# A float32 attention and mixture-of-experts kernel: the moving operand and the output of its split products are walked in pairs of columns

## The reference, cut to what matters

```python
q = query + braak_embed[braak_stages][..., None]
attn = softmax(einsum('bsd,btd->bst', q, key)); o = einsum('bst,btd->bsd', attn, value)
t = rms_norm(o) * norm_w
weights = top2(softmax(t @ gate_w.T))
h1 = (t @ w1.T)[None] + 2.0 * einsum('etr,efr->etf', einsum('td,erd->etr', t, a1), b1)
h3 = (t @ w3.T)[None] + 2.0 * einsum('etr,efr->etf', einsum('td,erd->etr', t, a3), b3)
act = silu(h1) * h3
out_e = einsum('etf,df->etd', act, w2) + 2.0 * einsum('etr,edr->etd', einsum('etf,erf->etr', act, a2), b2)
out = x + einsum('te,etd->td', weights, out_e)
```

## Time and profile before

| | |
|---|---|
| timed executions, median of 2 | 1308.16 us |
| profiled execution | 1308.66 us |
| its span | 1306.9 us |
| TensorE matmuls, records | 7286 |
| granted TensorE clock over the span | 1.00 of full speed |
| VectorE busy | 65% |
| ScalarE busy | 40% |
| DMA over the span | 53 GB/s |

### The profile page before, as it was taken

The page is one execution under the profiler, slowest core; times in us unless marked ns, Lnnn a source line. Parts: engine busy times, 40 slices in busy tenths (PEclk is TensorE's granted clock), DMA queues, the critical chain, the costliest instruction groups (busy, mean ns, idle before and its releaser), DMA issues.

```text
span 1306.9 us, 18607 instructions
## 1 busy us (share of the span) xinstructions
PE 1301.1 (100%) x7286; PEld 1139.3 (87%) x7286; DVE 843.5 (65%) x1558; ACT 527.5 (40%) x991; POOL 249.9 (19%) x213
## 2 busy tenths in 40 slices
PE   9999999999999999999999999999999999999998
PEld 8999998888888888888888888888888888888887
DVE  6776656756665576656675667557675666565556
ACT  6776753333343344333333334333333343243332
POOL 3556540202011020202020202011020202020200
PEclk9999999999999999999999999999999999999999
DMA  9555810020202020201102020202020101102000
GB/s 294 145 147 154 233 43 33 2 73 2 73 2 73 1 73 1 59 16 33 42 2 73 1 73 2 73 1 74 2 73 1 57 17 35 40 1 73 1 17 17
DMA packets 71791, 69.56 MB, mean 53 GB/s; under 512 B 7050, under 2 KB 62744, under 8 KB 71576
## 3 DMA queue, kind: packets, MB, share of 16 engines
q1 hardware_dynamic: 71392, 68.37, 17.5%
q10 hardware_dynamic: 312, 0.02, 0.0%
HBM read 51.27 MB, written 17.10 MB: 52 GB/s over the span
## 4 chain that ended last, share of the span: by engine, by line
PE 98%; ACT 1%; DVE 0%; issue 0%; DVEq 0%
PE bank L1205 31%; PE bank L1204 31%; PE bank L1206 30%; PE bank L1330 2%; PE bank L1257 2%; PE bank L1308 1%; PE bank L1250 1%; ACT prob L663 0%; PE bank L1216 0%; ACT qT_hi L646 0%; ACT kT_hi L647 0%; DVE probT_lo L886 0%; DVE x_out L1148 0%; PE bank L1295 0%; ACT value_hi L657 0%
## 5 line engine op out<-in xcount | busy, mean ns | idle before, releaser
L1076 DVE TENSOR_TENSOR act_a<-silu_a,bank 128x512 f32<-128x512 f32 x128 | 87.7, 686 | 210.9 <-PE bank L1206 194.2
L754 ACT ACTIVATE br_hi<-act_br 128x512 fp32r<-128x512 f32 x128 | 81.0, 633 | 188.6 <-DVE act_br L1087 188.6
L747 ACT ACTIVATE silu_b<-bank 128x512 f32<-128x512 f32 x128 | 76.3, 596 | 187.9 <-PE bank L1206 187.0
L590 POOL TENSOR_TENSOR t_lo<-t_in,t_hi 128x512 fp32r<-128x512 f32 x32 | 40.6, 1291 | 552.2 <-ACT t_hi L734 552.2
L1205 PE MATMUL bank<-w2T_lo,s_hi 128*128 128x256 f32 x512 | 144.7, 283 | 0.0
L1206 PE MATMUL bank<-w2T_hi,s_lo 128*128 128x256 f32 x512 | 143.3, 280 | 0.0
L1204 PE MATMUL bank<-w2T_hi,s_hi 128*128 128x256 f32 x512 | 142.7, 279 | 0.0
L1084 DVE TENSOR_TENSOR act_b<-silu_b,bank 128x512 f32<-128x512 f32 x128 | 88.0, 688 | 81.4 <-PE bank L1206 80.4
L743 ACT ACTIVATE silu_a<-bank 128x512 f32<-128x512 f32 x128 | 75.8, 592 | 134.1 <-PE bank L1206 134.0
L609 POOL TENSOR_TENSOR v_lo<-v_full,v_hi 128x512 fp32r<-128x512 f32 x64 | 94.5, 1508 | 136.6 <-ACT v_hi L739 136.6
L1097 DVE TENSOR_TENSOR br_lo<-act_br,br_hi 128x512 fp32r<-128x512 f32 x128 | 104.7, 818 | 5.6 <-ACT br_hi L754 3.1
(11 more groups left out here) (197 smaller groups left out, 3242.2 us busy)
## 6 DMA issues: line engine op xcount, KB each, us to landing
kv<-in_fside_BxSxS SPq DMA_DIRECT2D x32, 256.0 KB, 3.3
x_in<-in_x SPq DMA_DIRECT2D x32, 256.0 KB, 4.0
t_scratch<-oT SPq DMA_DIRECT2D x32, 256.0 KB, 2.5
t_in<-t_scratch SPq DMA_DIRECT2D x16, 512.0 KB
x_out<-in_x SPq DMA_DIRECT2D x16, 512.0 KB, 4.0
out<-x_out SPq DMA_DIRECT2D x30, 256.0 KB, 4.0
rho<-scale_scratch SPq DMA_DIRECT2D x16, 256.0 KB
rstd<-scale_scratch SPq DMA_DIRECT2D x16, 256.0 KB
```

Source lines behind the costliest of these rows:

```text
L747: nc.scalar.activation(silu_b[:, :], h1_bank[j % 2][:, :], ACT.Silu).then_inc(silu_b_ready, 1)
L754: nc.scalar.activation(br_hi[j % 2][:, :], act_br[j % 2][:, :], ACT.Copy).then_inc(br_hi_ready, 1)
L1076: nc.vector.tensor_tensor(act_a[j % 2][:, :], silu_a[j % 2][:, :], h3_bank[j % 2][:, :], ALU.mult).then_inc(act_a_ready, 1)
```

## The change

One line is added to `product`. The output and both parts of the moving operand are rearranged, all in the same way, before the three matmuls are issued. With N columns, the order becomes 0, 1, N/2, N/2 + 1, 2, 3, N/2 + 2, N/2 + 3, and so on: two neighbouring columns (8 bytes) of the first half, two of the second half, by turns. Since the output is walked in the same order as the moving operand, every value lands where it did before. The stationary operand and its load are as before.

```diff
             def product(dst, w, x_parts, start, stop, grouped=True):
 
                 (w_hi, w_lo), (x_hi, x_lo) = w, x_parts
+                dst, x_hi, x_lo = (part.rearrange("p (a b c) -> p b a c", a=2, c=2) for part in (dst, x_hi, x_lo))
                 nc.tensor.matmul(dst, w_hi, x_hi, start=start, stop=False, skip_group_check=not grouped)
                 nc.tensor.matmul(dst, w_hi, x_lo, start=False, stop=False, skip_group_check=not grouped)
                 return nc.tensor.matmul(dst, w_lo, x_hi, start=False, stop=stop, skip_group_check=not grouped)
```

## The result

The changed kernel took 1859.72 us (median of 2, 1859.07 to 1860.38) against 1308.16 us: ratio 1.421, 95% interval 1.418 to 1.425. It is slower by 42%, where 3.8% faster was forecast. Its profiled execution has a span of 1857.3 us, 550.4 us more than before.

What follows compares the result with a forecast made beforehand. TensorE's matmul distances were taken to bound the kernel; savings of 35.1, 2.8, 10.4 and 2.3 us summed to 50.6 us, bringing the median from 1308.16 to 1258 us, 3.8% faster. The range was 1238 to 1395 us.

Steps and rivals of the forecast that it cites:

- What bounds the kernel: Whole span: TensorE's matmul start distances set the time; excess over streaming the columns totals 81 us.
- Is the excess a fixed price or a stall: Matmuls in `product`: the 13.4 ns excess at 512 columns is mostly a stall between moving read and weight load.
- The read: Moving operand from SBUF: pairs by turns remove most of the stall, giving 218 ns for 512 columns, 111.5 for 256.
- The write: Product output to PSUM: writing pairs by turns costs 0, since two float32 values still stand together.
- The walk doesn't matter: Matmuls: excess is a price of changing weights under a moving stream; 1308 us, chance 0.27.
- The moving read takes every turn: TensorE reads: pairs take all memory turns, weight loads push the moving stream back; 1395 us, chance 0.20.
- Half the rate: SBUF read or PSUM write: memory takes one place per two turns; about 2400 us, chance 0.08.

Runs made afterwards that it cites:

- e7_same_place: Against the kernel before: the moving read takes the operand's first four columns (16 bytes) again and again, output written in order; 1249.25 us.
- e8_half_loads: Kernel before, with the middle matmul of each product loading and using 64 columns of weights instead of 128; 1319.27 us.
- g1_each_place_twice: Against the kernel before: the moving read takes each 16-byte place's four columns twice, walking only the operand's first half; 1247.51 us.
- f3_every_fourth: Against the kernel before: the moving operand is read as columns 0, 4, 8 and so on, then 1, 5, 9; output in order; 2528.95 us.
- e2_write_only: Against the kernel before: only the output is written in pairs by turns, the moving operand is read in order; 1307.09 us.
- e6_forward_pairs: Against the kernel before: moving columns read as 0, 1, 4, 5 and so on, then 2, 3, 6, 7; output in order; 2491.91 us.
- f2_forward_fours: Against the kernel before: moving columns read as 0 to 3, 8 to 11 and so on, then 4 to 7, 12 to 15; output in order; 1332.78 us.

## Why the prediction was wrong

**What bounds the kernel** was right, and so was the accounting: a change of distance passes to the time undiminished. The counts times the measured distances give the loss to 4 us. (They include 15 matmuls of `first_scores` and `last_down_z` that didn't change, under 1 us.) No other engine came near the path, in either direction.

**"Is the excess a fixed price or a stall"** was half right. The excess can be lost (`e7_same_place`: 215.7 ns, the floor of 215.6 that was worked out from the transposes). But that the stall lies between the moving read and the weight load was only argued, from an uneven row and a plausible picture. `e8_half_loads` speaks against it without settling it, `g1_each_place_twice` fits it as well as its rival, and no walk by turns went faster than the walk in order. A stall that depends on where the read is may have its cause in that read alone; where it lies stays open. Even without the stall the forecast's lowest time of 1239 us was out of reach: `e7_same_place` took 1249.25 us, since its matmuls of 256 columns took (738.46 - 735.78) / 24 = 111.7 ns and not 109. The gain of 50.6 us rested on this step and on the next.

**"The read" is the step that failed**, and it alone decides the sign. It was priced at nothing from the weight load of `w2_in`, which opens a place about every 0.83 ns at no cost. Two things differ from the case it was taken for: it is the other read of TensorE, and it takes one column from each place. The second is enough, as `f3_every_fourth` shows for the moving read: one column per place goes at 0.90 ns a column there, near the weight load's 0.85. For the weight load that is as fast as its walk in order, for the moving read it is half as fast, and taking a second column from the place doesn't help: 0.88 ns a column in the forward pairs. So the row gave a rate of places, while what held in the runs was a rate of columns. The term of the sum was set at 218 ns between bounds of 215.6 and 436 and is 333.3, which adds 4032 x 106.6 ns = 430 us where a gain of 35 was forecast; for 256 columns 111.5 ns was set and 170.4 measured.

**"The write"** was set at 0 and is 0 (`e2_write_only`, 1307.09 us). Here the Trainium skill's rule in "PSUM — Partial Sum Buffer", section Specifications, that a non-contiguous pattern slows matmuls, does not hold for pairs; what "Advanced Engine Details and Errata", section Memory Cachelines, says of PSUM, that every two consecutive elements should be contiguous, agrees. The prediction called that section the milder one, but it has the strict rule as well, and the same run speaks against it there. The same section's line on SBUF, two hits for each 16-byte line, is what the prediction let stand, and it is not enough on this read: two hits leave 451 ns, four give 233 (`e6_forward_pairs`, `f2_forward_fours`).

**The rivals.** "The walk doesn't matter" was wrong. "The moving read takes every turn" had the right side, but put the price on the weight load's reads and so at 13 ns a matmul, where it is 106.6. "Half the rate", at 0.08, is the nearest to what came: one place for each pair at half the rate, on the SBUF side, though its 2400 us were not met either. It would have been met to 4%, with 451 ns and 2492 us where it had 436 and 2400, had the walk only gone forward. It was left outside the range because the weight load's row was allowed to speak against it. What it lacked is that a place stays held while one other is visited, which halves the loss: 106.6 ns instead of 224.

**The chances.** An untried access pattern on the operand that sets the time had one row on its side, and that from the other read of TensorE. 0.45 for a gain was too much for that, and the half rate should have been in the range.

## What to carry to other kernels

When a stream sets the time, ask how many consecutive columns it takes from each place it opens, and price a new pattern by a row of the same read with the same number of columns per place; without such a row keep the whole range. In these runs a float32 moving operand wants four consecutive columns, the 16 bytes of a place, before it leaves (233.3 ns against 451 with two); the output in PSUM was content with two. And a stall whose cause is only argued is no ground for a gain. Runs that change the suspected cause alone come first: here the half load and the one place would have shown that 11 ns can be lost, but not by a shorter load.

## What the runs showed of the hardware

- Each matmul of 512 columns in the walk in order pays 11 ns over the 215.7 of one place, which go if each place gives eight columns instead of four (216.0). No walk tried here that reads each column once does better than in order.
- The moving read takes 0.88 ns a column when each place gives two columns and 0.90 when it gives one, against 0.44 in order: with one or two columns from a place it runs at half the rate.
- TensorE's moving read holds two places: two fixed ones by turns cost 1 ns in all (216.7 against 215.7). With four moving ones it pays nearly the full price (443.3 against 451).
- Leaving a fully read place for a distant one isn't free either: 23 ns for fours by turns, 17 for eights (both with the write by turns as well), 6.6 for fours that skip forward. Why, is open. So is why a second place 252 columns away is 13 ns dearer than 256, why one column from a place costs as much as each of two, and what the 11 ns of the walk in order consist of.
- Writes to PSUM in pairs by turns are free at the rate of the walk in order (9.52 us for the 42 matmuls with and without them).
